# Attention over a window: scores on 146 of 164 keys, three short mask products, and TensorE products into an unused bank

## The reference

```
q = (x @ Wq + bq) ...            # 12 heads, 16 wide; k and v likewise
scores = einsum('bhqd,bhkd->bhqk', q, k) * SCALE
allowed = abs(idx[:, None] - idx[None, :]) <= 64
scores = where(allowed, scores, -inf)
attn = softmax(scores)
out = einsum('bhqk,bhkd->bhqd', attn, v) ... @ Wo + bo
```

## Time and profile before

| | |
|---|---|
| median of 3 runs | 2430.45 us (2428.31 to 2439.93) |
| span of the profiled execution | 2436.7 us |
| TensorE products, busy | 2309.0 us, 95% of the span |
| VectorE, busy | 1892.6 us, 78% |
| ScalarE, busy | 1407.7 us, 58% |
| mean granted TensorE clock | 0.966 |
| attention, first to last TensorE product | 331.5 to 882.3 us |
| spline layers | 891.5 us to the end |

### The profile page before, as it was taken

How to read it: one execution, slowest core, us unless ns; L and a number is a source line. 1 busy time by engine, 2 the same in 40 slices (tenths; PEclk the granted TensorE clock), 3 DMA queues, 4 the chain that set the end, 5 groups by cost and what they waited for, 6 DMA issues and landing times.

```text
span 2436.7 us, 49389 instructions
## 1 busy us (share of the span) xinstructions
PE 2309.0 (95%) x20297; PEld 2155.4 (88%) x20297; DVE 1892.6 (78%) x2364; ACT 1407.7 (58%) x1391; POOL 229.4 (9%) x132
## 2 busy tenths in 40 slices
PE   7699959999999969999999999989999999999999
PEld 6366848888888859999999999989999999999999
DVE  8699745666666668676676766679999999999995
ACT  5588113444444374443534435488888888888881
POOL 5422000000000003121121211000000000000000
PEclk9799967999999969999999999999999999999999
DMA  7655130111111100000000001120000000000000
GB/s 242 164 150 149 55 145 22 44 45 45 44 45 45 45 22 20 26 19 15 26 19 26 19 15 34 64 84 23 23 23 23 23 23 23 23 23 23 23 18 10
DMA packets 99328, 116.26 MB, mean 48 GB/s; under 512 B 15271, under 2 KB 90423, under 8 KB 98487
## 3 DMA queue, kind: packets, MB, share of 16 engines
q1 hardware_dynamic: 79087, 89.38, 12.2%
q10 hardware_dynamic: 16520, 14.75, 2.0%
q0 software_dynamic: 3616, 10.54, 1.7%
HBM read 83.77 MB, written 30.86 MB: 47 GB/s over the span
## 4 chain that ended last, share of the span: by engine, by line
PE 63%; issue 0%; DVE 0%
PE spline_acc L1890 26%; PE spline_acc L1863 10%; PE spline_acc L1862 9%; PE spline_acc L1864 9%; PE spline_acc L1884 5%; PE spline_acc L1886 2%; PE spline_xT L761 0%; DVE spline_f L1639 0%; DVE spline_weights_low L1622 0%; DVE spline_x L1709 0%; DVE spline_x L1712 0%
## 5 line engine op out<-in xcount | busy, mean ns | idle before, releaser
L1890 PE MATMUL spline_acc<-spline_weights,spline_f 128*128 128x192 f32 x3936 | 672.0, 328 | 0.0
L1890 PEld LDWEIGHTS spline_acc<-spline_weights,spline_f 128*128 128x128 f32 x3936 | 637.2, 190 | 0.0
L1863 PE MATMUL spline_acc<-spline_f,spline_weights_high 128*128 128x328 f32 x1536 | 482.7, 314 | 0.0
L1862 PE MATMUL spline_acc<-spline_f,spline_weights_high 128*128 128x328 f32 x1536 | 480.1, 313 | 2.5 <-DVE spline_weights_low L1622 2.5
L1864 PE MATMUL spline_acc<-spline_f,spline_weights_low 128*128 128x328 f32 x1536 | 476.5, 310 | 0.0
L1862 PEld LDWEIGHTS spline_acc<-spline_f,spline_weights_high 128*128 128x128 f32 x1536 | 290.2, 189 | 2.8 <-DVE spline_weights_low L1622 2.8
L1863 PEld LDWEIGHTS spline_acc<-spline_f,spline_weights_high 128*128 128x128 f32 x1536 | 289.3, 188 | 0.0
L1864 PEld LDWEIGHTS spline_acc<-spline_f,spline_weights_low 128*128 128x128 f32 x1536 | 288.9, 188 | 0.0
L1884 PE MATMUL spline_acc<-spline_weights_split,spline_f_high 128*128 128x384 f32 x656 | 218.2, 389 | 8.2 <-issue 8.2
L1639 DVE SCALAR_TENSOR_TENSOR spline_f<-spline_front 128x984 fp32r<-128x984 f32 x128 | 145.5, 1177 | 100.7 <-PE spline_acc L1864 95.0
L1019 DVE TENSOR_REDUCE attend_max<-scores_by_query 82x6 f32<-82x984 f32 x128 | 150.8, 1178 | 67.8 <-PE scores_by_query L1334 67.8
(11 more groups left out here) (224 smaller groups left out, 4286.6 us busy)
## 6 DMA issues: line engine op xcount, KB each, us to landing
spline_front<-pos_scr SPq DMA_DIRECT2D x32, 540.0 KB, 4.4
hid_scr<-spline_hid SPq DMA_DIRECT2D x64, 164.0 KB, 1.8
spline_xn<-hid_scr SPq DMA_DIRECT2D x41, 256.0 KB, 3.1
attend_spread<-rec_scr SPq DMA_DIRECT2D x128, 61.5 KB, 2.2
pix_scr<-spline_front SPq DMA_DIRECT2D x32, 225.0 KB
spline_weights_raw<-w SPq DMA_DIRECT2D x1, 6144.0 KB, 21.3
spline_weights<-w SPq DMA_DIRECT2D x4, 1536.0 KB, 6.3
spline_x<-h_scr SPq DMA_DIRECT2D x41, 96.0 KB, 1.9
```

Source lines behind the costliest of these rows:

```text
L1862: nc.tensor.matmul(z, high, x_high, start=start, stop=False)
L1863: nc.tensor.matmul(z, high, x_low, start=False, stop=False)
L1890: last = nc.tensor.matmul(z, f_rest[i][:, cols], w2[:, i, r, :], start=False, stop=stop)
```

## The change

Scores are made on the 146 keys (`SPAN`) that a chunk of 82 can reach, keys 0 to 145 for chunk 0 and 18 to 163 for chunk 1, and likewise by key on 146 queries. The maximum, the maximum product and the exponential cover 146 columns of each head group instead of 164. `mix` takes all 164 queries for the first key chunk (18 of them from zeros that a new memset writes once to `prT`) and 146 for the second. The window is added with three products of 96, 96 and 108 columns: two edges of 32 columns and one for the two corners of 18. Their weights are slices of a new `piecer`, in which row 0 covers all rows ahead of the edge.

`keep_going(n, spare)` is new. It issues n products with 128 x 128 weights and 384 columns into a bank that holds nothing then; nobody reads them. TensorE issues 48 ahead of the wait for the memsets, 8 after the first `turn_x`, 9 after each of the first four query passes, 18 ahead of the first pair's query pass 1, 20 in `finish` after its output projection, and 28 after each of the last two output projections. The memsets are now six, and TensorE waits for them after its first 48 products.

```diff
-        self.piecer = sb("window_piece_r", [P, self.PIECES, ROWS], F32R)
-        self.maskr = sb("window_mask_r", [P, 2, self.PIECES, TOK], F32R)
+        self.piecer = sb("window_piece_r", [P, 2, SPAN], F32R)
+        self.maskr = sb("window_mask_r", [P, 2, EDGE], F32R)
...
+            pool.memset(prT[0:ROWS, 0, :, SPAN:TOK], 0.0).then_inc(zeros_set, 1)
...
-                                        sc[0:ROWS, :, 0:SC].rearrange("p j (g n) -> p j g n", n=TOK),
+                                        sc[0:ROWS, :, 0:SW].rearrange("p j (g n) -> p j g n", n=SPAN),
...
-                nc.scalar.activation(prT[0:ROWS, c].rearrange("p (j g) n -> p j (g n)", j=4), tp[0:ROWS, :, 0:SC],
+                nc.scalar.activation(prT[0:ROWS, c, :, FROM[c]:FROM[c] + SPAN].rearrange("p (j g) n -> p j g n", j=4),
+                                     tp[0:ROWS, :, 0:SW].rearrange("p j (g n) -> p j g n", n=SPAN),
...
-            pe.wait_ge(zeros_set, 5)
-
...
+            def keep_going(n, spare):
+
+                for _ in range(n):
+                    nc.tensor.matmul(spare, wqh[:, 0, 0:P], wkh[:, 0, :], start=True, stop=True)
...
-                            nc.tensor.matmul(sc[0:ROWS, j, g * TOK:(g + 1) * TOK],
+                            nc.tensor.matmul(sc[0:ROWS, j, g * SPAN:(g + 1) * SPAN],
                                              q1[u][r, g, i * TOK + n * ROWS:i * TOK + (n + 1) * ROWS],
-                                             k[r, g, i * TOK:(i + 1) * TOK],
+                                             k[r, g, i * TOK + FROM[n]:i * TOK + FROM[n] + SPAN],
...
-                for p, cols in WINDOW[n]:
+                for p in range(3):
                     for row, bank in tiles:
                         r = slice(32 * row, 32 * row + 32)
-                        last = nc.tensor.matmul(
-                            scores[0:ROWS, bank, 0:SC].rearrange("p (g n) -> p g n", n=TOK)[:, :, cols],
-                            piecer[r, p, :],
-                            maskr[r, n, p:p + 1, cols].to_broadcast([32, HG, cols.stop - cols.start]),
-                            start=False, stop=(stop and (p, cols) == WINDOW[n][-1]))
+                        of = scores[0:ROWS, bank, 0:SW].rearrange("p (g n) -> p g n", n=SPAN)
+                        if p < 2:
+                            at = WINDOW + 32 * p if n == 0 else CORNER + 32 * (1 - p)
+                            to = of[:, :, at:at + 32]
+                            edge = maskr[r, n:n + 1, 0:32].to_broadcast([32, HG, 32])
+                        else:
+                            rows, groups = of.ap[0], of.ap[1]
+                            to = bass.AP(tensor=of.tensor, offset=of.offset,
+                                         ap=[list(rows), list(groups), [SPAN - CORNER, 2], [1, CORNER]])
+                            edge = maskr[r, n:n + 1, 32:EDGE].rearrange("p a (s n) -> p a s n", s=2
+                                                                        ).to_broadcast([32, HG, 2, CORNER])
+                        at = WINDOW - 32 * p if n == 0 else 32 * p
+                        last = nc.tensor.matmul(to, piecer[r, n, at:at + ROWS], edge, start=False,
+                                                stop=(stop and p == 2))
...
-                        last = nc.tensor.matmul(tp[0:ROWS, j, g * TOK:(g + 1) * TOK], pickr[r, g, :], mT[r, :],
+                        last = nc.tensor.matmul(tp[0:ROWS, j, g * SPAN:(g + 1) * SPAN], pickr[r, g, :],
+                                                mT[r, FROM[c]:FROM[c] + SPAN],
...
+                        n = slice(0, TOK) if c == 0 else slice(FROM[c], TOK)
...
-                                                prT[0:ROWS, c, HG * j + g, :],
+                                                prT[0:ROWS, c, HG * j + g, n],
...
                 project_out(a - 2, 1, use(t, Y_LAST[1]))
+                keep_going(20, tp[:, 0, 0:HG * P])
...
+                        if first and q == 1 and i == 0:
+                            keep_going(18, xb[:, claim(use(t, X[0])), 0:HG * P])
...
+            keep_going(48, tp[:, 0, 0:HG * P])
+            pe.wait_ge(zeros_set, 6)
             for j in range(2):
                 turn_x(0, j, start(START["X"][j]))
+            keep_going(8, tp[:, 0, 0:HG * P])
...
             for q in range(4):
                 queries_scores(0, 0, 0, q, True)
+                keep_going(9, tp[:, 0, 0:HG * P])
...
             for i in range(2):
                 project_out(2 * PAIRS - 2 + i, i, use(PAIRS, Y[i]))
+                keep_going(28, tp[:, 0, 0:HG * P])
```

More of the change, by code:

```diff
@@ L39 @@
 ROWS = TOK // 2
+WINDOW = 64
+SPAN = ROWS + WINDOW
+CORNER = TOK - SPAN
+EDGE = 32 + 2 * CORNER
 PAIRS = B // 2
@@ L822, in attend_phase @@
     SC = HG * TOK
-    PIECES = 3
-    WINDOW = ([(p, slice(64 + 32 * p, TOK)) for p in range(PIECES)] + [(2, slice(0, 18))],
-              [(p, slice(0, min(50 + 32 * p, TOK - 64))) for p in range(PIECES)] + [(0, slice(TOK - 18, TOK))])
+    SW = HG * SPAN
+    FROM = (0, CORNER)
     NX = 16
@@ L998, in _ @@
         def _(dve):
-            dve.wait_ge(zeros_set, 5)
+            dve.wait_ge(zeros_set, 6)
             def norm_in(tt, u):
@@ L1378, in mix @@
                     for j in range(4):
-                        last = nc.tensor.matmul(xb[32 * j:32 * j + 32, bank, g * TOK:(g + 1) * TOK],
+                        n = slice(0, TOK) if c == 0 else slice(FROM[c], TOK)
+                        last = nc.tensor.matmul(xb[32 * j:32 * j + 32, bank, g * TOK + n.start:(g + 1) * TOK],
                                                 va[u][0:ROWS, 2 * i + c, 4 * g + j, :],
-                                                prT[0:ROWS, c, HG * j + g, :],
+                                                prT[0:ROWS, c, HG * j + g, n],
                                                 start=(c == 0 and g == 0), stop=(c == 1 and g == HG - 1))
@@ L1993, in layouts @@
     w = {k: np.asarray(v) for k, v in i.items() if k.startswith("L0_attn")}
-    at = np.arange(32)[:, None, None, None] + ROWS * np.arange(2)[:, None, None] + 32 * np.arange(3)[:, None]
-    dist = np.abs(at - np.arange(TOK)) * (at - ROWS * np.arange(2)[:, None, None] < ROWS)
-    to = np.arange(32)[:, None, None] + 32 * np.arange(3)[:, None]
+    row, col = np.arange(32)[:, None], np.arange(SPAN)
+    piece = np.where(row == 0, col < WINDOW, col == row + WINDOW - 1)
+    edge, corner = np.arange(32), np.arange(CORNER)
+    mask = np.concatenate([edge >= row, corner <= row - 2, corner >= row], 1)
+    mirror = np.concatenate([mask[:, 31::-1], mask[:, :31:-1]], 1)
     wo = np.zeros((4, 32, HG, D), f32)
```

17 lines of the change are left out of this document (8 added, 9 removed).

## The result

The changed kernel takes 2422.7 us (median of 20 runs, 2410.62 to 2446.39) against 2440.21 us for the kernel before in the same runs (20, 2428.31 to 2449.07): ratio 0.9941, 95% interval 0.9926 to 0.9955. It is 17.5 us faster by the medians (0.7%; 0.6% by the ratio, which is clear of noise). The forecast was 2382 us (2364 to 2407) and 48 us faster; the direction was right, the time lies outside the range, and two thirds of the saving are missing. The profiled run took 2410.74 us with a span of 2409.0 us, the second lowest time of the 20. Each ratio in this document is against the kernel before, timed beside the kernel in question.

The account below looks back on a forecast made before the run. TensorE was taken to set attention's pace, with waits in every pair. Steady pairs 28, start 16, end 3 and constants 1 sum to 48 us, off the 2430.45 us median: 2382 us, range 2364 to 2407.

Parts of the forecast that it names:

- start: Attention's first pairs, to 403 us: products into an empty bank keep the clock up, 16 us saved; 21 with clock kept.
- end: Attention's last stretch: shorter passes save, extra products fit the waits; 3 us, from 6 gained to 5 lost.
- constants: Offset phase before attention: a smaller mask load ends it sooner, worth 1 us (0 to 1.5).
- Few falls, one to three: 2390 to 2406 us: Rival, chance 0.07: less TensorE work and longer waits make the clock fall in steady pairs, about 8 us a fall.
- the steady sum: Steady pairs: what the waits give back sums to 2.0 us a pair, 28 us over 14 pairs.
- the rivals of more falls: Steady pairs: six or more clock falls eat the 48 us, chance 0.04; four or five, or an unseen cost, 0.04.
- The walk by its steps: A steady pair followed by what comes last at each point, adding the gains: 2.0 us a pair.
- at the first: From the last K projection's end to the first wait for the maximum: VectorE sets the time, gain 0.11 us.
- at the second: From the first to the second wait for the maximum: query products, masks, latency and maximum, gain 0.33 us.
- at the third: From there to the transposed maximum: two query passes, values and a mix without a wait, gain 0.54 us.
- at the fourth: The transposed maximum's chain through ScalarE, VectorE and TensorE: gain 0.
- at the fifth: Query passes and one key pass save 0.98 us, but the Q projection's wait for split x limits the gain to 0.73.

Follow-up runs that it names:

- e4: Changed kernel with the mask's load padded back to 492 KB, the padding unread: 2416.8 us, ratio 0.9913.
- e12: Changed kernel again, unedited, with a second trace: ratio 0.9912, median of all eight runs 2427.57 us.
- e15: Changed kernel again, unedited, a further trace: 2424.74 us.
- e16: Changed kernel again, unedited, one more trace: 2434.17 us.
- e1: Changed kernel without any keep_going products, only the 146 keys and short masks left: 2427.23 us, ratio 0.9964.
- e2: Kernel before with all the keep_going products, 164 keys and four mask steps kept: 2433.36 us, ratio 0.9977.
- e5: Changed kernel plus four and two products ahead of the second and third query passes of each pair's second image, into a free bank: 2405.18 us, ratio 0.9881.
- e6: Changed kernel plus two products ahead of the second query pass of each pair's second image, into a free bank: 2413.97 us, ratio 0.9903.
- e8: Changed kernel plus four products ahead of the second query pass of each pair's second image, into a free bank: 2406.81 us, ratio 0.9874.
- e17: Changed kernel plus four and two products in steady pairs, twelve in a first-pair wait, 28 there for 18, more in the last pair: 2397.9 us, ratio 0.9835.
- e9: Changed kernel plus four products in steady pairs, twelve in a first-pair wait, 28 there for 18, more in the last pair: 2405.48 us, ratio 0.9886.
- e10: Changed kernel without its own keep_going products, but with four in each steady pair's wait: 2423.97 us, ratio 0.9926.
- e3: Changed kernel plus four and two products ahead of the second and third query passes of each pair's second image, into a bank still being read: 2426.04 us, ratio 0.9953.

## Why the prediction was wrong

The means over traces, three of the kernel before against five with the changed kernel's attention (first trace, e4, e12, e15, e16), in us:

```
            before   changed   saved   forecast
start        77.3      65.6     11.7     16
13 pairs    401.0     398.1      2.9     26 (13 x 2.0)
end          80.0      77.9      2.1      5 (3, and pair 15's 2)
constants                        0        1
sum                             16.7     48
```

The timed medians differ by 17.5 us. That the two agree to 1 us is partly luck: the spans of these eight traces differ by 19.9 us in the mean, 3 of them outside attention, and what lies ahead of the sampling varies by 12 us with the kernel unchanged. Of the 31 us that are missing, 18 went to the falls with the late sums, 5 to steady pairs that save less than forecast, 4 to the start, 3 to the end and 1 to the constants.

- **The step that failed: "Few falls, one to three: 2390 to 2406 us", with a chance of 0.07, and the steady sum that left them out.** The rival was right in mechanism and in its place: the shorter passes bring the falls (e1 has them, e2 with the inserted products alone has none), and with the wait filled they are gone (e5, e6, e8, e17), but for those behind late sums (e9, e10). Its weight was wrong, 0.15 with the rivals of more falls: the kernel before had no fall in 39 steady pairs of three traces, and the changed one 16 in 65, two to five a trace. At 29.22 us the 13 pairs would take 379.9; they took 398.1. The falls, and the late sums with them, cost 18.2 us. I priced a fall at 8 us, with one to three of them; in the changed kernel's first trace three falls, 37.5 us at half clock, cost 16.5. Three falls in place of none would have given 2406 us by my price, so the falls alone don't account for the measured time. That a clock of 1.00 over 440 us meant room to spare was my error. The earlier trace rows showed that it held, not by how much.
- **Products, mis-sized.** The period fell by 1.63 us, not 2.0: 22.8 us over 14 pairs for 28. The walk by its steps: 4.88 to 4.77 us at the first (0.11 forecast, 0.11 measured), 0.28 for 0.33 at the second, 0.45 for 0.54 at the third, 0 at the fourth, 0.46 for 0.73 at the fifth. The rest of the pair gave 0.33 for 0.30. A mask group takes 0.20 us for 0.16 by the starts of its products and 0.22 by those of its loads. What I had wrong is the pace of the weight loads. In the key passes of the steady pairs at full clock, in the changed kernel's first trace, the loads of four row groups start within 10 ns of each other, but the next round starts 73 ns later, in the score steps (146 columns) and in the mask steps (96 and 108) alike; in the kernel before no round follows in under 70 ns. So a mask step can't go to 53 ns, and a score step lost 3 ns for 7.5: rounds of 76 ns became rounds of 73. I was wrong to argue from sixteen loads in 0.33 us that a step could go lower: they are four rounds, of 83 ns in the mean. By the section "LDWEIGHTS (loading the stationary operand)" of the Trainium skill's "TensorE: Matmul & The Clock Gate", loading 82 columns takes 68 ns; the trace's 73 ns come near it.
- **Start.** 11.7 us for 16. The 48 products took 10.39 us (11.2 forecast) and didn't delay the first transpose. The clock fell in the 2.09 us wait at 370.06 us, the one at 389.01 before, as forecast. To the point where the forecast's stretch ends (402.99 us before, 382.28 changed) the first traces give 14.1 us for 16. The part that is short is the first one, to the transposed maximum: 2.4 us for 4.5. The projections took 11.6 us for 12.9 before, with 3.4 us of them at half clock, and the four query passes stand 2.58 us apart for 2.3: nine products take 1.7 to 1.8 us there, for 1.56 forecast. The rest, to 384.76 before (365.93 changed), is 9.8 us for 10.0; in e16 the clock fell once more, behind the 18 products, and the start took 70.99. Of the gain, e1 shows 6.9 us for narrowing alone, e2 2.5 us for the products alone: by these single traces they give more together than their sum. e17 with all waits filled has a start of 58.4 us.
- **End.** 2.1 us for 5; the 28 products (5.17 us) pushed nothing back.
- **Constants.** Priced from one trace's pauses in the offset phase; e4 shows nothing.
- **Right:** the length of the reduction and the exponential, the longer waits for the maximum, and the fall in the first pair. Of the signs that I had named for being wrong, "a half clock between 420 and 800 us" came in every trace of the changed kernel. Of those for being right, mask groups of 0.16 us and a period near 28.9 didn't come (0.20 and 29.22), and the clock was at 1.00 from 329.9 to 370.8 us, near the 331 to 375 that I had named. The first transpose came later than 332 us in three of the five traces, but in one of the three of the kernel before as well, so that sign told nothing.

What is open: how many falls an execution has isn't settled by anything in the kernel that I found; the traces had two to five. They are most of the spread, though: over the 20 executions the time rises by 0.44 us with each us at half clock (correlation 0.91). And the share of the late sums among the falls is from few cases: three of 16, all in e15 and e16, plus both of e10 and one behind e9's steady pairs.

## What to carry to other kernels

When an edit takes work from an engine whose clock depends on its activity, and there are waits in its loop, count the clock as part of the price: the row that shows full clock doesn't say how near the edge it is. If the edge is reached, products that nobody reads, in the wait itself and into a bank whose last reader is long done, are nearly free: four cost nothing in the steady pairs and gave some 9 to 16 us here (ratio 0.9874 against 0.9941, and 0.9912 in e12, whose interval overlaps); in a bank still being read they cost as much as they give. A forecast from a single trace should ask what varies between executions: here the start of the sampling moved by 12 us and the falls by 41 us of half clock with the changed kernel's attention as it was.

## What the runs showed of the hardware beyond that

- The granted clock can fall behind a recorded wait of 0.65 us, in one pair and not in the next with the same timeline: 13 of 16 falls stood 18.9 to 20.3 us behind their pair's first transpose, at the same query pass, and the 16 lasted 10.2 to 17.1 us each. It doesn't fall in e3's waits of 1.1 us, which have four full-width products behind them.
- Half clock costs less than its length: 12.0 us for 27.3 (e1), 16.5 for 37.5 (changed kernel), 0.44 of it; 0.44 to 0.50 in the other four traces of the changed kernel's attention, late sums included.
- Weight loads of 82 columns, four row groups side by side, start every 73 ns when the products between them have 96 to 146 columns (full clock, the changed kernel's trace), and never under 70 ns apart in the kernel before, whatever the columns.
- A load of 7.7 KB that was never late at a period of 30.85 us (65 pairs) is waited for, by up to 1.8 us, in one to three of 13 pairs once the period is 29.2 to 29.5 (none in e17).
